# The opening of a convolution and MLP kernel: transfers on the sync queue in another order, and nine unused matmuls on TensorE

## The reference, cut to what matters

```python
def _L0_cond_ref(u, length, log_dt, C, log_A_real, A_imag, D):
    mask = (jnp.arange(Lq) < length[:, None]).astype(u.dtype)
    u_m = u * mask[:, None, :]
    kernel = _get_kernel(log_dt, C, log_A_real, A_imag, Lq)
    ...
    y = jnp.fft.irfft(u_f * k_f, n=n)[..., :Lq]
    y = y + u_m * D[:, None]
    return y * mask[:, None, :]
def _L1_cond_ref(x, W_gate, W_up, W_down, A_gate, ..., lora_indices, layer_idx):
    gate = lora_add(jnp.einsum('bnh,fh->bnf', x, W_gate), x, A_gate, B_gate)
    up = lora_add(jnp.einsum('bnh,fh->bnf', x, W_up), x, A_up, B_up)
    act = jax.nn.silu(gate) * up
    down = lora_add(jnp.einsum('bnf,hf->bnh', act, W_down), act, A_down, B_down)
    return down
x = x + _L0_cond_ref(x, itok_B_8_3872, ...)
x = x + _L1_cond_ref(x, ..., itok_B_2_6, 0)
```

## Time and profile before

| what | value |
|---|---|
| median of 3 runs | 559.6 us (558.12 to 559.83) |
| the profiled execution, its own time | 559.0 us |
| its span | 557.3 us |
| TensorE matmul busy | 519.2 us, 93% |
| weight load busy | 472.5 us, 85% |
| VectorE, ScalarE, GpSimd busy | 256.3, 200.5, 39.8 us |
| mean granted TensorE clock over the span | 0.995 of full |
| moved by transfers | 53.19 MB, 95 GB/s over the span |

### The profile page before, as it was taken

The page is one execution under the profiler, slowest core; times in us unless marked ns, Lnnn a source line. Parts: engine busy times, 40 slices in busy tenths (PEclk is TensorE's granted clock), DMA queues, the critical chain, the costliest instruction groups (busy, mean ns, idle before and its releaser), DMA issues.

```text
span 557.3 us, 10115 instructions
## 1 busy us (share of the span) xinstructions
PE 519.2 (93%) x3169; PEld 472.5 (85%) x3169; DVE 256.3 (46%) x556; ACT 200.5 (36%) x427; POOL 39.8 (7%) x55
## 2 busy tenths in 40 slices
PE   0097899999999999999999999999999999999997
PEld 0097787989898989999898989898989898999986
DVE  7873267544444434353435353534444443435341
ACT  6790008333333433242323233323333343324221
POOL 1006700100000000000000000000000000000000
PEclk9999899999999999999999999999999999999999
DMA  7899991312030404030304031211203040404000
GB/s 275 284 339 390 319 315 48 73 56 69 28 99 9 115 0 120 4 111 13 111 13 107 16 93 31 84 39 54 69 25 98 8 116 0 120 3 111 13 21 19
DMA packets 32306, 53.19 MB, mean 95 GB/s; under 512 B 7586, under 2 KB 16194, under 8 KB 32290
## 3 DMA queue, kind: packets, MB, share of 16 engines
q1 hardware_dynamic: 32290, 53.00, 31.9%
HBM read 48.69 MB, written 4.28 MB: 95 GB/s over the span
## 4 chain that ended last, share of the span: by engine, by line
PE 86%; DVE 5%; DMA 5%; ACT 1%; issue 1%; SPq 0%; DVEq 0%
PE ps_g L982 21%; PE ps_u L982 20%; PE ps_db L1020 13%; PE ps_da L1020 13%; PE ps_x L1011 3%; PE ps_x L962 3%; PE ps_g L936 2%; DMA toep<-kpad 2%; DMA kpad<-k_sb 2%; PE ps_u L936 2%; PE ps_g L992 2%; PE ps_u L992 2%; PE ps_g L993 2%; PE ps_u L993 2%; PE ps_x L1054 1%
## 5 line engine op out<-in xcount | busy, mean ns | idle before, releaser
L475 ACT CAST b_spl<-b_raw 64x512 fp32r<-64x512 f32 (+1 forms) x96 | 54.6, 570 | 98.6 <-PE ps_u L993 79.3
L800 DVE TENSOR_TENSOR b_spl<-b_raw,b_spl 64x512 fp32r<-64x512 f32 (+1 forms) x96 | 60.4, 630 | 53.8 <-ACT b_spl L475 50.1
L982 PE MATMUL ps_g<-w_hi,x_hi 128*128 128x512 f32 (+1 forms) x192 | 72.7, 379 | 1.4 <-DVE x_lo L894 1.4
L982 PE MATMUL ps_u<-w_hi,x_hi 128*128 128x512 f32 (+1 forms) x192 | 71.4, 372 | 0.0
L982 PE MATMUL ps_u<-w_lo,x_hi 128*128 128x512 f32 (+1 forms) x192 | 71.3, 371 | 0.0
L982 PE MATMUL ps_u<-w_hi,x_lo 128*128 128x512 f32 (+1 forms) x192 | 71.3, 371 | 0.0
L982 PE MATMUL ps_g<-w_lo,x_hi 128*128 128x512 f32 (+1 forms) x192 | 71.1, 370 | 0.0
L982 PE MATMUL ps_g<-w_hi,x_lo 128*128 128x512 f32 (+1 forms) x192 | 71.0, 370 | 0.0
L836 DVE TENSOR_TENSOR h_act<-h_act,ps_u 128x512 f32<-128x512 f32 (+1 forms) x48 | 30.4, 633 | 54.1 <-PE ps_u L993 54.0
L1020 PE MATMUL ps_da<-wd_hi,ht_hi 128*128 128x288 f32 (+1 forms) x176 | 54.6, 310 | 0.0
L1020 PE MATMUL ps_db<-wd_hi,ht_hi 128*128 128x288 f32 (+1 forms) x176 | 53.3, 303 | 0.0
(11 more groups left out here) (167 smaller groups left out, 917.8 us busy)
## 6 DMA issues: line engine op xcount, KB each, us to landing
a_raw<-atab SPq DMA_DIRECT2D x64, 152.0 KB, 2.5
toep<-kpad SPq DMA_DIRECT2D x16, 512.0 KB, 7.7
b_raw<-btab SPq DMA_DIRECT2D x128, 64.0 KB, 2.1
um<-xr SPq DMA_DIRECT2D x16, 256.0 KB, 5.3
x<-xT SPq DMA_DIRECT2D x8, 512.0 KB, 6.8
w_raw<-wgu SPq DMA_DIRECT2D x8, 512.0 KB, 9.2
out<-y_sb SPq DMA_DIRECT2D x15, 256.0 KB, 2.1
b_raw<-btab SPq DMA_DIRECT2D x64, 44.0 KB, 1.8
```

The lines of the kernel that those rows point to most:

```text
L475: nc.scalar.copy(b_spl[0:LR, up, 0:w], b_raw[slot][:, up * w:(up + 1) * w]).then_inc(b_hi, 1)
L800: V.tensor_tensor(b_spl[LR:P, up, 0:w], b_raw[slot][:, up * w:(up + 1) * w], b_spl[0:LR, up, 0:w].bitcast(F32), ALU.subtract).then_inc(b_l ...
L982: T.matmul(ps[:, 0:w], xs[:, q, kb, :], ws[:, kb, col:col + w], start=(kb == 0 and xs is x_hi and ws is w_hi), stop=False)
```

## The change

The prologue's queue is reordered. x(1,0) and x(1,1) come ahead of pieces 4 and 5; pieces 6 to 11 are spread between the Toeplitz loads; the halves of x(2) and x(3) move; a moves from behind pair 8 to behind pair 11, and b from behind pair 9 to behind pair 13. `load_um(4)` now stands ahead of `store_taps(1)`. On VectorE the length mask moves from behind taps(0) to behind taps(1). On TensorE nine matmuls of 256 columns (`ident` against `um` slot 0, into `ps_x[0]`, which nobody reads before it is overwritten) stand between taps(0) and conv(0). They wait only for um 0.

```diff
@@ sync engine @@
             load_x(0, 1)
-            for n in range(2 * KB):
+            for n in range(KB):
                 load_piece(n)
+            load_x(1, 0)
+            load_x(1, 1)
+            load_piece(KB)
+            load_piece(KB + 1)
             sp.wait_ge(idx_in, 16)
             ids0 = indices(0, 0)
             sp.wait_ge(zero_out, 16)
             store_taps(0)
-            load_piece(2 * KB)
             for pair in range(RC):
                 load_toep(pair, pair, 0)
-            for n in range(2 * KB + 1, NP_GU):
-                load_piece(n)
-            load_x(1, 0)
+            load_piece(KB + 2)
+            load_piece(KB + 3)
+            load_x(2, 0)
+            load_um(RC, 0, False)
             store_taps(1)
-            load_x(1, 1)
-            load_x(2, 0)
-            for pair in range(RC, 2 * RC):
+            load_x(2, 1)
+            load_toep(RC, 0, 1)
+            load_piece(2 * KB)
+            for pair in (RC + 1, RC + 2):
                 load_um(pair, pair - RC, False)
                 load_toep(pair, pair - RC, 1)
-                if pair == RC:
-                    load_x(2, 1)
-                if pair >= RC + 2:
-                    store_taps(pair - RC)
-                    load_x(3, pair - RC - 2)
+            store_taps(2)
+            load_piece(2 * KB + 1)
+            load_um(RC + 3, 3, False)
+            load_toep(RC + 3, 3, 1)
+            store_taps(3)
+            load_piece(2 * KB + 2)
...
                 load_um(pair, pair % RC, False)
                 load_toep(pair, pair % RC, pair // RC)
                 if pair == 2 * RC:
+                    load_piece(2 * KB + 3)
+                if pair in (2 * RC + 1, 2 * RC + 2):
+                    load_x(3, pair - 2 * RC - 1)
+                if pair == 2 * RC + 3:
                     load_a(0, 0, ids0)
-                if pair == 2 * RC + 1:
+                if pair == 3 * RC + 1:
                     sp.wait_ge(mask_done, KB + 1)
                     load_b(0, 0, 0, ids0)
@@ VectorE @@
             taps(0)
-            for i in range(KB + 1):
-                length_mask_step(i)
             phases(1)
             phases(2)
             tables(1)
             phases(3)
             taps(1)
+            for i in range(KB + 1):
+                length_mask_step(i)
@@ TensorE @@
+            def keep_busy():
+                pe.wait_ge(um_in[0], 16)
+                for i in range(9):
+                    T.matmul(ps_x[0][:, 0:KB * NB], ident[:, :], um[:, 0, 0:KB * NB], start=True, stop=True)
+
             taps(0)
+            keep_busy()
             conv(0)
```

## The result

The change makes the kernel slower, by about 0.4%. The median of 20 runs is 560.32 us (558.82 to 563.26), against 558.88 us (556.84 to 560.59) in 20 runs of the kernel before on the same chip: a ratio of 1.0038 [1.0025, 1.0052]. I had forecast 556.6 with a range of 554.6 to 558.9. The profiled execution took 559.91 us, its span is 558.1 (557.3 before), and its mean granted clock 0.997.

What follows compares the result with a forecast made beforehand. Transfers in the first 80 us, ahead of the first MLP matmul, bound it. toep 0 at 26.7, a 46.4 to 46.8 us stretch and two convolutions save 3.0; 559.0 less 3.0 plus 0.6 is 556.6, range 554.6 to 558.9.

Steps and rivals of the forecast that it cites:

- The start: Prologue up to toep 0: first store lands in 1.52 us, toep 0 takes 4.6 and lands at 26.7.
- Does the earlier store fill the hole: Transfers at 34 to 37 us: little; the second store lands at 35.3, the hole is kept at 1.3 us.
- The nine matmuls: TensorE ahead of conv(0): 2304 columns ending at 27.0, then conv(0) at the high clock ends at 29.4, not 32.7.
- The stretch: Transfers from toep 0's landing to toep 15's: 46.4 us in place of 46.9, so toep 15 lands at 73.1.
- sum by parts: The stretch as 16.5 MB: 0.88 in 4 us at 221 GB/s, 15.6 at 377, hole 1.3: 46.8 us.
- the other way: The stretch from its earlier 46.9 us, plus 1.0 for piece 8, less 1.5 for the slow late part: 46.4 us.
- a sign of being wrong: End of the stretch: the prediction is wrong if toep 15 lands later than 75 us.
- piece 8's 0.36: In the stretch: piece 8, which stood ahead of toep 0, adds 0.36 MB, 1.0 us.
- Covered edits: Later x(3), pieces 8 to 11, a and b hold up nothing; GpSimd's remainders slip to some 72 us.
- Slower: Rival: queue shallow everywhere, 317 GB/s for the whole stretch, toep 15 at 78.8; 2.5 us slower, 562.1; chance 0.06.
- Rival 1: Clock stays low after the nine matmuls or falls in a late convolution's wait; gain 1.2 us, 558.4; chance 0.13.
- Rival 2: Order gains nothing, only bytes count: 344 GB/s, toep 15 at 75.6, gain 0.7 us, 558.9; chance 0.12.

Runs made afterwards that it cites:

- f1: The changed kernel itself, unaltered, run again beside three variants on one chip: 560.79 us, 1.0053 against the kernel before.
- e1: The changed kernel without its nine unused matmuls, a still late: 559.59 us, 1.0006 against the kernel before.
- f4: The changed kernel without the nine matmuls and with a behind pair 8 again: 556.96 us, 0.9975 against the kernel before.
- the square: Four runs on one chip: the changed kernel with or without the nine matmuls, a late or early; 556.96 to 560.79 us.
- e10: The changed kernel with a behind pair 8 again and five unused matmuls of 512 columns in place of nine of 256: 557.18 us, 0.9980.
- e11: The changed kernel with a behind pair 8 again and both halves of x(2) behind the second store, nine matmuls kept: 556.61 us, 0.9968.
- e9: The changed kernel without the nine matmuls, a behind pair 8 again, both halves of x(2) behind the second store: 557.08 us, 0.9981.
- e12: The changed kernel without the nine matmuls, a behind pair 8 again, the length mask back behind taps(0): 557.2 us, 0.9975.
- e2: The kernel before with the nine unused matmuls added and nothing else of the change: 558.22 us, 0.9981.
- f2: The changed kernel without the nine matmuls, a late, the same kernel as e1: 559.93 us, 1.0024 against the kernel before.
- e4: The changed kernel with the four stores of taps issued by ScalarE on its own queue: 562.76 us, 1.0064 against the kernel before.

## Why the prediction was wrong

**The start was right, in part by luck.** toep 0 landed at 26.43 (26.7 forecast), but two misses cancelled: the first store took 2.0 us (1.52), and toep 0 took 3.8 us from issue: between the row's 4.6 and the estimate of 3.2 worked out from the Trainium skill's page, so that neither was exact. The nine matmuls ended at 25.36 (27.0; at 26.2 in f1, the same kernel), conv(0) took 2.62 us, so the clock had risen in them, and the store was issued at 31.83 (31.9).

**"Does the earlier store fill the hole": the term was copied, not worked out.** I saw that 3.4 MB stood ahead of the store and put its landing at 35.3. Without the nine matmuls it landed at 35.7 (e1), so that step was good; with them, at 37.3 (36.9 in f1). The hole was a term I copied ("I keep the hole as it was", 1.3 us for three windows of 1 us) and it measured 2.2 over 36 to 39 us. In f4, with neither the nine nor the late a, the same three (55, 231 and 209 GB/s) give 1.7. The gap opens when all that is queued has moved and closes when toep 4's bytes flow. Before, two x halves and um 4 stood behind the store; now one half does, so there is little to bridge a late landing, and the nine matmuls' delay of the store, 1.0 to 1.4 us in the square's profiles, goes into the hole in part.

**"The nine matmuls": priced on TensorE alone.** Their term was columns and clock, and it came out right. The cost lay elsewhere: 0.9 to 1.1 us by the square, where the first MLP matmul came 0.76 and 0.84 us later with them. It seems to go with the number of instructions (e10); its mechanism stays open. No row of the kernel before priced it, but the page has the instruction queue's line, and I never asked when its packets come.

**"The stretch" was too kind.** It took 49.3 us, where my sum by parts had 46.8 (46.4 the other way); toep 15 landed at 75.76, past the 75 that I had set as a sign of being wrong. The last row of the windows is 350 GB/s over 49.33, 17.3 MB where I counted 16.5: 2.1 us. The hole is 0.9 more (2.2 for 1.3). b costs a little less than it did: 4 us at 256 GB/s lack 1.3 us, where 4 us at 221 lacked 1.7. Together 2.6, for the 2.5 that it took longer. The 333 GB/s at 65 to 75 us are b's stretch, which lay at 57 to 61 before. (My words "the small b rows" were wrong too: each of its 64 KB transfers brings 16 rows of 4 KB. Why it runs slowly is open.) Where the extra bytes come from, windows from the start to toep 0's and to toep 15's landing tell. Before and changed, up to toep 15:

```profile
0.00:74.57 74.57, 42.67 (x291) 39.51 (x292) 43.89 (x143) 33.13 (x69) 21.12 (x25) 0.98 0.94 320
```

```profile
0.00:75.76 75.76, 47.90 (x319) 43.28 (x320) 47.41 (x145) 33.33 (x69) 21.60 (x25) 0.98 0.92 323
```

That is 23.9 and 24.5 MB. All that stands ahead of toep 15 is the same in both, so the 0.6 MB more come from behind it: the down pieces. toep 15 was issued 3.1 us sooner than before, at 66.84, and still landed later, 8.9 us after its issue; the down pieces are issued from 67.26 and share the engines with it. Up to toep 0's landing the two kernels moved 7.7 and 7.2 MB, so 0.5 MB had to pass later, of which I counted piece 8's 0.36. The term that I had at nothing is what is queued behind the last load.

**"Covered edits": the step that cost most.** "The later a delays GpSimd's remainders of pieces 4 to 7 to some 72, and they are wanted 8 us behind the first MLP matmul." The second half held: in the changed profile nothing in the MLP waits for them. The first was 5 us short: the remainders ran to 77.29, since a's four transfers were issued from 54.69 on and took 8.0 us to land, so that GpSimd could pack a only at 65.48 (56.97 before), and the remainders come behind that. Done by 72, they would have been clear of the split of b at 75.11. And I asked only who needs the result, not what else works while it is made. The groups of those lines in the changed kernel (durations in ns, min/median/max):

```profile
L810 DVE TENSOR_TENSOR b_spl<-b_raw,b_spl x2: 676/1702/2727, 75.1 to 77.8; 64x512 fp32r<-64x512 f32 x2
```

```profile
L395 POOL TENSOR_TENSOR w_lo<-w_raw,w_hi x4: 2349/3000/3017, 66.0 to 74.3; 128x1024 fp32r<-128x1024 f32 x4
```

The first of the two splits starts at 75.11, while GpSimd's last instruction runs from 74.3 to 77.29, and takes 2.73 us: it ends at 77.84, 0.55 behind GpSimd's end. The second takes 0.68. So it looks as if it waited for the whole of GpSimd's instruction and did its own work then. The remainders on VectorE, which also read two tensors in SBUF, fit: beside GpSimd two of them took 2.12 and 1.30 us in place of 0.87, and the one at 74.19, which began ahead of GpSimd's instruction at 74.3, took 0.90. The Trainium skill ("SBUF — State Buffer", section "Who interferes with whom") has this: a VectorE instruction with two inputs in SBUF and a GpSimd one that reads SBUF exclude each other, and whichever comes first holds the port to its end. Both of these read two tensors in SBUF, and the rows agree; the additions of the convolutions, which read PSUM, kept their 0.74 us beside the same GpSimd work.

By the square this step accounts for 2.8 to 3.0 us, as much as the whole gain I had forecast: 1.4 us of wait and, in many executions, a fall of the clock behind it, 1.6 us. The nine matmuls account for about 1. Of my 3.0, the new order alone keeps 1.5 (f4: 558.42 less 556.96).

**The rivals.** "Slower" came true, but not by my mechanism: the queue was not shallow at 317 GB/s from end to end (350 over the stretch, and 333 to 395 in the windows above but for the one from 34 to 37 us). I gave it 0.06. Rival 1 saw the clock fall in a wait, but among the convolutions: it did fall at 43 to 46 us (0.50, below) and cost little: f1, the same kernel, had no fall there, and its first MLP matmul came 0.48 us sooner, when its toep 0 had been issued 0.51 sooner. The fall that cost was behind the last convolution, where I had taken the idleness to be fixed. Rival 2, that only bytes count, came nearest for the transfers: 344 GB/s and toep 15 at 75.6 (350 and 75.76 measured). Its 558.9 left out what came behind the convolutions.

```profile
43.00:46.40 3.40, 3.08 (x11) 2.62 (x10) 0.73 (x1) 0.52 (x1) 3.40 (x2) 0.50 1.04 347
```

**The best version** is e11: the changed order with a behind pair 8, both halves of x(2) behind the second store, and the nine matmuls: 556.61, 0.9968 [0.9952, 0.9985], where the change as made is 1.0038. Its lead over e9, e10 and e12, on the same chip, is 0.5 to 0.6 us, and the intervals of the ratios overlap.

## What to carry to other kernels

When a load is moved, follow its consumer in time, not only to the one who wants its result: list what every other engine does in the new place, VectorE against GpSimd above all. The gap at a dependent store depends on what is queued ahead of it and behind it, so it has to be worked out anew for each order; it can't be carried over. What stands behind the last load that matters shares the engines with it, and counts. Unused instructions are priced on their engine, and it is worth looking at what they move on the DMA engines, which bring in the program. A longer idle time ahead of a full stretch is priced with the clock that may fall behind it.

## What was not expected of the hardware

- GpSimd and VectorE at work together: a VectorE instruction of 0.68 us took 2.73, and GpSimd's of 2.35 took 3.00.
- A 16 KB store issued from ScalarE's queue took 6.7 us, and from the sync queue at the same time 5.5. Over the orders tried the second store took 1.8 to 6.7 us for the same 16 KB: 1.8 in e9, and 4.0 in e11, which adds the nine matmuls alone.
- A fetch of 16 KB of instructions began at 42 us in the kernel before and at 34 with nine more matmuls (e2); in the new order at 39 without them (e1) and at 33 with them, and at 34 with five wide ones (e10).
- The four transfers of b, 256 KB, come with a stretch of some 4 us at 221 to 256 GB/s in which the DMA share is 1.06, in the kernel before and, 10 us later, in the changed one.
- After 2.75 to 2.78 us of idleness the clock fell in three profiles (e1, f1, f2), always just behind the restart and not in the idle time, and after 2.77 us in e4 and 2.58 us in the changed kernel's own profile it did not. In the kernel before, ahead of conv(9), it fell within the 2.67 us of idleness (0.64 over 60 to 61 us).
